# Gated cross-attention and mixture of experts: the reads of the transposed head outputs moved within a slot, ahead of the second pair's exps on ScalarE and ahead of statistics and routing on VectorE

## The chip, the cores and the metric

The kernel runs on 1 core of one Trainium2 chip. The metric is the device time of one execution in microseconds (us), the median of several runs. The time before is 597.08 us (3 runs, 595.59 to 599.96).

## The reference, cut to what matters

Two batches of 1024 tokens of 256 features pass through a gated cross-attention to 154 context rows each (16 heads of 64) and then a gated mixture of experts with top 2 of 8 experts. The kernel works the attention in float32 split in a high and a low part, so that nearly every product is three matmuls.

```python
q = x @ Wq; k = context @ Wk; v = context @ Wv            # 16 heads of 64
attn = softmax(einsum('bhid,bhjd->bhij', q, k) * SCALE)
out = einsum('bhij,bhjd->bhid', attn, v)
x = x + tanh(g_xattn[0]) * (out @ Wo + bo)                # x went in layer-normed
...
logits = clip(xf @ router_w.T, -CLAMP, CLAMP)             # xf: layernorm of layernorm
topk_p, topk_i = top_k(softmax(logits), 2)
x = x + tanh(g_ffn[0]) * sum over chosen experts of down(silu(gate) * up)
```

## The kernel before, in words

**Two phases.** The first phase (a `Block` from L246) does attention and, behind it, routing: it writes the rows chosen for each expert to a queue in HBM. The second phase (L1196 on) runs 39 tiles of 128 queued rows through the experts. The change touches the first phase alone, which takes the first 340 us or so.

**Slots.** The 16 token tiles of 128 rows are worked in NI = 4 iterations of 4 tiles. An iteration has 16 slots, u = 0 to 15, and a slot is one tile's step over four heads (HQ = 4), so a tile takes four slots (UPT = 4). Iteration 0 and iteration 3 are written out, 1 and 2 are passes of a hardware loop (`Fori(1, NI - 1)`). Each engine runs its own `slot(i, u)` with an order of work written by hand, and the engines meet only through semaphores. Everything on one engine is done in the order of its text.

**A slot on TensorE** (L652 to L691) issues: the first half of the scores of slot u + 2 (L543; needs the exps of the first pair of heads of slot u + 1 to be done); the five transposes of the probabilities of slot u (L557); in even slots the four transposes of half of a finished tile's head outputs, `transpose_out` (L590, into a PSUM bank of `O_BANK`); the second half of the scores of slot u + 2 (needs the exps of the second pair of slot u + 1); probabilities times values of slot u - 1, `attend` (L581); a projection job of the next tiles in slots with u % 8 of 0, 1, 2, 4, 5 (L516 and L527, `JOB_SLOT`); `project_out` in slots with u % 4 = 3 (L603, 24 matmuls). The `attend` of an even slot u, which stands in slot u + 1, overwrites the bank that `transpose_out` filled, so it waits on `ot_sb`: for VectorE's read of that bank. In slot 15 the transposes L557 first wait for `pos_read`, the end of VectorE's `count_rows` (L1013), since they overwrite the counts.

**A slot on ScalarE** (L792 to L808): exps of the first pair of heads of slot u + 2 (L773, two activations and their accumulator reads); copy of the transposed probabilities (L800); exps of the second pair of slot u + 2; in even slots `transposed_out` (L779, the cast L782 of the transposed head outputs into `oT_hi`); the high part of a job (L761, L764).

**A slot on VectorE** (L1041 to L1076): the first pair's maxima of slot u + 2 (L892); in odd slots `scale_out` (L901, L903); copy of the rest of the transposed probabilities (L1056); the second pair's maxima; then `block_stats` (u % 4 = 0, L931, L933), `token_stats` (u % 8 = 2, L861, L864), `normalise` (u % 8 = 7), `route_step` (u = 5, 6: `norm_stats` L941, L944; u = 7, 8: `start_output` L970; u = 12, 13: `choose` L997 to L1005), `count_rows` (u = 14, L1010 and L1013); then in even slots `transposed_out` (L911, the subtraction L916 into `oT_lo`, after ScalarE's L782); the low part of a job (L880, L885); the residual (L923) in slots with u % 4 = 3. Iteration 0 has no routing and no `transposed_out` before slot 4.

**Behind it.** GpSimd works the norms of routing (L384 to L407), adds the output bias (L368) and sends rows. In slot 9 TensorE transposes the routed features (L611), ScalarE and VectorE copy them in slot 10 (L786, L974), and the transposes L557 of slot 10 wait for both copies.

Of the kernel before, what the change touches and what calls it, by code (L numbers as in the profile page):

```python
# [47 lines left out]
def gated_xattn_moe(nc, x, ctxT, g_x, g_f, Wq, Wk, Wv, Wo, bo, gamma, beta, rwT, guT, dnT, out):  # L48
# [14 lines left out]
    UPT = H // HQ  # L63
# [25 lines left out]
    with ExitStack() as ctx:  # L89
# [88 lines left out]
        with ExitStack() as actx:  # L178
# [568 lines left out]
            def _(act):  # L747
# [31 lines left out]
                def transposed_out(i, u):  # L779
                    half = (u % UPT) // 2  # L780
                    act.wait_ge(s["ot_ps"][half], TPI * i + u // UPT)
                    nc.scalar.copy(oT_hi[:, 4 * half:4 * half + 4, :].rearrange("p c t -> p (c t)"), O_BANK[half][:, :]).then_inc(s["ot_hi"][half], 1)  # L782

                def turned_features(i):
                    act.wait_ge(s["xfT_ps"], 2 * i - 1)
                    nc.scalar.copy(xfT[:, 0:4, :].rearrange("p c t -> p (c t)"), TA[:, :]).then_inc(s["xfT_sb"][0], 1)  # L786
# [5 lines left out]
                def slot(i, u):  # L792
                    first = isinstance(i, int) and i == 0
                    last = isinstance(i, int) and i == NI - 1
                    if not first and u == TURN + 1:
                        turned_features(i)
                    ahead = exps(i, u + 2) if not (last and u + 2 >= UPI) else iter(())
                    next(ahead, None)
                    act.wait_ge(s["ptA"], UPI * i + u + 1)
                    nc.scalar.copy(pT[u % 2][:, 0:3, :].rearrange("p b t -> p (b t)"), TA[:, 0:3 * P]).then_inc(s["ptA_sb"], 1)  # L800
                    next(ahead, None)
                    if u % 2 == 0 and not (first and u < UPT):
                        transposed_out(i, u)
                    w, g = u % 8, GPI * i + u // 8 + 1
                    if w in JOB_SLOT and not (last and u >= 8):
                        high_part(g, JOB_SLOT[w], JOB_BANK, (u // 8 + 1) % 2)
                    if not first and u == LOGIT + 1:
                        router_exp(i)  # L808
# [14 lines left out]
                for u in range(UPI):  # L823
                    slot(0, u)
# [20 lines left out]
            def _(dve):  # L845
# [65 lines left out]
                def transposed_out(i, u):  # L911

                    half = (u % UPT) // 2
                    part = slice(4 * half, 4 * half + 4)
                    dve.wait_ge(s["ot_hi"][half], TPI * i + u // UPT)
                    nc.vector.tensor_tensor(oT_lo[:, part, :].rearrange("p c t -> p (c t)"), O_BANK[half][:, :],  # L916
                                            oT_hi[:, part, :].rearrange("p c t -> p (c t)").bitcast(F32), ALU.subtract).then_inc(s["ot_sb"][half], 1)
# [123 lines left out]
                def slot(i, u):  # L1041
                    first = isinstance(i, int) and i == 0
                    last = isinstance(i, int) and i == NI - 1
                    w, g = u % 8, GPI * i + u // 8 + 1
                    if not first:
                        route_step_early(i, u)
                    ahead = maxima(i, u + 2) if not (last and u + 2 >= UPI) else iter(())
                    next(ahead, None)
                    if not first and u == LOGIT + 1:
                        shifted_logits(i)  # L1050
                    if not first and u == LOGIT + 2:
                        router_probs(i)
                    if u % 2 == 1 and not (first and u < 2):
                        scale_out(i, u - 2)
                    dve.wait_ge(s["ptB"], UPI * i + u + 1)
                    nc.vector.tensor_copy(pT[u % 2][:, 3:5, :].rearrange("p b t -> p (b t)"), TB[:, 0:2 * P]).then_inc(s["ptB_sb"], 1)  # L1056
                    next(ahead, None)

                    if u % UPT == 0 and u // UPT >= 2:
                        block_stats(i + 1, u // UPT - 2)  # L1060
                    elif u % UPT == 0 and not first:
                        block_stats(i, u // UPT + 2)
                    if w == 2 and not last:
                        token_stats(i + 1, u // 8)
                    if w == 7 and not last:
                        normalise(i + 1, u // 8)
                    if not first:
                        route_step(i, u)
                        if u == COUNT:
                            count_rows(i)  # L1070
                    if u % 2 == 0 and not (first and u < UPT):
                        transposed_out(i, u)
                    if w in JOB_SLOT and not (last and u >= 8):
                        low_part(g, JOB_SLOT[w], JOB_BANK, (u // 8 + 1) % 2)
                    if w % UPT == UPT - 1 and not (first and u < UPT):
                        add_residual(i, u)  # L1076
# [386 lines left out]
```

## Time and profile before

| what | us |
|---|---|
| median of 3 runs | 597.08 |
| the three runs | 597.08, 599.96, 595.59 |
| span of the profiled execution, from its first to its last instruction | 602.2 |
| TensorE busy | 522.3 (87%) |
| VectorE busy | 340.4 (57%) |
| ScalarE busy | 282.2 (47%) |
| GpSimd busy | 231.9 (39%) |

For the profiled execution the page gives the span and no other time. All durations below are from that one execution, core 0, with times counted from the start of its span. PE is TensorE's matmuls, PEld its weight loads, DVE VectorE, ACT ScalarE, POOL GpSimd. In a timeline row the first number is the start, the second the duration, and a bracket at the end tells how long the engine had been idle and what released it. A duration runs from the start to the end of the write, and the next instruction of the same engine can start up to 0.1 us before that end.

### The profile page before, as it was taken

How to read it: one execution, taken by the hardware profiler on the slowest of the kernel's cores; microseconds unless marked ns; L12 is line 12 of the kernel's file. 1: busy time of each engine (PE TensorE's matmuls, PEld its weight loads, DVE VectorE, ACT ScalarE, POOL GpSimd, SP SyncE). 2: the span in 40 equal slices, each digit the busy share in tenths (PEclk: the TensorE clock that was granted, in tenths of full speed). 3: DMA queues.
4: the chain of work that ended last, by engine and by line, in shares of the span. 5: the costliest groups of instructions: out<-in, count | busy, mean ns of one | idle time of the engine just before them, and what ended most of it. 6: DMA issues, size and time to landing. Idle time of an engine off the chain costs nothing.

```text
span 602.2 us, 12363 instructions
## 1 busy us (share of the span) xinstructions
PE 522.3 (87%) x3712; PEld 476.4 (79%) x3713; DVE 340.4 (57%) x783; ACT 282.2 (47%) x866; POOL 231.9 (39%) x319
## 2 busy tenths in 40 slices
PE   8999999999999999998998420699988998999991
PEld 6789999998989889898998410588877877888881
DVE  5856666677586585765756764255444544533330
ACT  3446556555465555564553112355543544533330
POOL 5160000337008780077704625043433433443333
PEclk9999999999999999999999755799999999999995
DMA  8500000001000100001010995636446436333322
GB/s 246 181 2 1 0 2 2 20 1 35 3 0 26 44 20 15 0 10 63 2 36 1 224 229 178 206 84 151 109 90 156 117 76 157 53 51 53 55 36 26
DMA packets 32372, 41.54 MB, mean 69 GB/s; under 512 B 3088, under 2 KB 28432, under 8 KB 32336
## 3 DMA queue, kind: packets, MB, share of 16 engines
q1 hardware_dynamic: 25184, 31.75, 17.9%
q0 software_dynamic: 7152, 9.33, 9.9%
q8 instruction: 21, 0.34, 0.2%
q14 instruction: 15, 0.12, 0.1%
HBM read 24.12 MB, written 16.95 MB: 68 GB/s over the span
## 4 chain that ended last, share of the span: by engine, by line
PE 34%; issue 26%; DVE 11%; ACT 8%; DMA 6%; POOL 6%; POOLq 3%; DVEq 2%; SPq 2%; another core or an unknown queue 1%; ACTq 0%
PE bank L603 7%; PE bank L581 6%; ACT probs L773 5%; PE bank L527 4%; POOL tok L1225 4%; PE bank L543 4%; PE bank L1279 3%; PE bank L557 3%; DMA expert_queue<-zrow 3%; DVE nmax L892 2%; POOLq L1233 2%; DMA out_dram<-yq,to_row 2%; PE bank L706 2%; PE bank L501 2%; DVEq L902 1%
## 5 line engine op out<-in xcount | busy, mean ns | idle before, releaser
L773 ACT ACTIVATE probs<-bank,nmax 128x154 f32<-128x154 f32 x256 | 97.6, 388 | 123.6 <-DVE nmax L892 119.3
L581 PE MATMUL bank<-vdiag,pT 128*128 128x128 f32 (+2 forms) x640 | 80.0, 272 | 7.1 <-DVE oT_lo L916 6.9
L581 PEld LDWEIGHTS bank<-vdiag,pT 128*128 128x128 f32 (+1 forms) x640 | 77.5, 191 | 10.5 <-DVE oT_lo L916 10.3
L1234 POOL DMA_INDIRECT out_dram<-yq,to_row x39 | 61.8, 1585 | 33.7 <-issue 24.1
L1279 PE MATMUL bank<-gu_hi,xqT_hi 128*128 x156 | 68.7, 441 | 1.1 <-DVE xqT_lo L1396 1.1
L892 DVE TENSOR_REDUCE nmax<-bank 128x2 f32<-128x308 f32 x128 | 60.1, 471 | 7.7 <-PE bank L543 6.8
L1279 PE MATMUL bank<-gu_hi,xqT_lo 128*128 x156 | 61.9, 397 | 0.0
L1279 PE MATMUL bank<-gu_lo,xqT_hi 128*128 x156 | 61.7, 396 | 0.0
L1408 DVE TENSOR_TENSOR hidT_lo<-bank,hidT_hi 128x512 fp32r<-128x512 f32 x39 | 26.9, 690 | 53.1 <-ACT hidT_hi L1355 53.1
L1403 DVE TENSOR_TENSOR hid<-hid,bank 128x512 f32<-128x512 f32 x39 | 26.8, 688 | 52.6 <-PE bank L1279 52.6
L557 PE MATMUL bank<-ident,probs 128*128 128x128 f32 (+1 forms) x320 | 46.2, 273 | 5.6 <-ACT xfT L786 2.9
L773 ACT ACTIVATION_READ_ACCUMULATOR probs<-bank,nmax 128x1 f32 x256 | 50.9, 199 | 0.0
L1232 POOL TENSOR_TENSOR to_row<-tok,no_offset 128x1 uint32<-128x1 uint32 x39 | 12.4, 317 | 95.0 <-DMA out_dram<-yq,to_row 90.8
L543 PE MATMUL bank<-k_hi,q_hi 128*128 128x308 f32 x128 | 46.8, 366 | 1.6 <-issue 1.0
L368 POOL TENSOR_TENSOR x<-x,bo_b 128x256 f32<-128x256 f32 (+1 forms) x16 | 12.4, 797 | 91.3 <-DVE xn L871 91.2
L1299 PE MATMUL bank<-dn_hi,hidT_hi 128*128 x156 | 44.4, 284 | 2.2 <-DVE hidT_lo L1408 2.2
L1362 ACT ACTIVATE yq<-bank,tgf 128x256 f32<-128x256 f32 x39 | 18.5, 475 | 55.7 <-DMA out_dram<-yq,to_row 53.8
L1299 PE MATMUL bank<-dn_lo,hidT_hi 128*128 x156 | 44.4, 284 | 0.0
L1299 PE MATMUL bank<-dn_hi,hidT_lo 128*128 x156 | 44.4, 284 | 0.0
L557 PEld LDWEIGHTS bank<-ident,probs 128*128 128x128 f32 (+1 forms) x320 | 37.3, 138 | 7.9 <-ACT xfT L786 3.6
L1262 PE MATMUL bank<-ident,xq 128*128 128x128 f32 x78 | 16.0, 287 | 27.6 <-DMA xq<-expert_queue 27.4
L543 PE MATMUL bank<-k_hi,q_lo 128*128 128x308 f32 x128 | 38.9, 304 | 0.0
(183 smaller groups left out, 1432.4 us busy)
## 6 DMA issues: line engine op xcount, KB each, us to landing
gu_raw<-in_gate_up_wT_dram SPq DMA_DIRECT2D x8, 1024.0 KB, 5.0
expert_queue<-zrow SPq DMA_DIRECT2D x8, 642.5 KB
xq<-expert_queue SPq DMA_DIRECT2D x39, 128.5 KB, 2.5
dn_raw<-in_down_wT_dram SPq DMA_DIRECT2D x8, 512.0 KB, 6.0
x<-in_x_dram SPq DMA_DIRECT2D x4, 512.0 KB, 13.0
out_dram<-out SPq DMA_DIRECT2D x8, 256.0 KB, 2.2
wq_raw<-in_L_xattn_Wq_dram SPq DMA_DIRECT2D x1, 1024.0 KB, 11.5
wo_raw<-in_L_xattn_Wo_dram SPq DMA_DIRECT2D x1, 1024.0 KB, 10.6
```

Source lines behind the costliest of these rows:

```text
L527: last = nc.tensor.matmul(at[:, m * GT:(m + 1) * GT], w[:, c, cols], v[:, c, :], start=(n == 0), stop=(n == 5))
L543: last = nc.tensor.matmul(S_BANK[hf][:, 0:2 * NKB], q[par][:, pair, tok:tok + P], k[:, pair, par, :], start=(n == 0), stop=(n == 2))
L557: last = nc.tensor.transpose(dst, probs[u % 4][:, b * P:b * P + rows], ident[:, :])
L581: last = nc.tensor.matmul(at[:, col0 + j0 * DH:col0 + j0 * DH + n], pT[u % 2][0:rows, b, :], v, start=(b == 0), stop=(b == NBLK - 1), skip ...
L603: last = nc.tensor.matmul(M_BANK[1][:, 0:D], o[:, c, :], w[:, c, :], start=(n == 0), stop=(n == most - 1))
L773: last = nc.scalar.activation(probs[u % 4][:, j * NKB:(j + 1) * NKB], S_BANK[hf][:, m * NKB:(m + 1) * NKB], ACT.Exp, bias=nmax[:, u % 4, j ...
L892: nc.vector.tensor_reduce(nmax[:, u % 4, 2 * hf:2 * hf + 2], S_BANK[hf][:, 0:2 * NKB].rearrange("p (m k) -> p m k", m=2), AX_X, ALU.max, n ...
L1234: nc.gpsimd.indirect_dma_start(out[:, :], bass.IndirectOffsetOnAxis(to_row[:, 0:1], 0), yq[p % 2][:, :], None, compute_op=ALU.add).then_in ...
L1279: last = nc.tensor.matmul(at[p % 2][:, :], rows[:, c, :], weights(w, rank, c * FF2 + half * FF, FF), start=(n == 0), stop=(n == 3 * KD - 1))
L1299: last = nc.tensor.matmul(Y_BANK[p % 2][:, 0:D], h[:, c, :], weights(w, rank, c * D, D), start=(n == 0), stop=(n == 3 * KF - 1))
L1403: nc.vector.tensor_tensor(hid[p % 2][:, :], hid[p % 2][:, :], U_BANK[p % 2][:, :], ALU.mult).then_inc(s["e_hid"], 1)
L1408: nc.vector.tensor_tensor(hidT_lo[:, :, :].rearrange("p c t -> p (c t)"), HT_BANK[:, :], hidT_hi[:, :, :].rearrange("p c t -> p (c t)").bi ...
```

## The change

On both engines the read of the transposed head outputs comes earlier in an even slot. On ScalarE it now stands between the copy L800 and the second pair's exps. On VectorE it now stands directly behind the second pair's maxima, ahead of `block_stats`, `token_stats`, `normalise`, `route_step` and `count_rows`. No instruction is added or removed, no semaphore changes, and TensorE's and GpSimd's programs stay as they are.

```diff
@@ ScalarE, slot(i, u) @@
                     nc.scalar.copy(pT[u % 2][:, 0:3, :]..., TA[:, 0:3 * P]).then_inc(s["ptA_sb"], 1)
-                    next(ahead, None)
                     if u % 2 == 0 and not (first and u < UPT):
                         transposed_out(i, u)
+                    next(ahead, None)
                     w, g = u % 8, GPI * i + u // 8 + 1
@@ VectorE, slot(i, u) @@
                     next(ahead, None)
 
+                    if u % 2 == 0 and not (first and u < UPT):
+                        transposed_out(i, u)
                     if u % UPT == 0 and u // UPT >= 2:
                         block_stats(i + 1, u // UPT - 2)
...
                         if u == COUNT:
                             count_rows(i)
-                    if u % 2 == 0 and not (first and u < UPT):
-                        transposed_out(i, u)
                     if w in JOB_SLOT and not (last and u >= 8):
```

## Rows read from the trace of the kernel before

**Rows 1.** Waits of PE from 42 to 326 us: total, times, longest.

```profile
PE bank L581 <- DVE oT_lo L916: 6.9, 12, 1.4
PE bank L557 <- ACT xfT L786: 2.9, 3, 1.2
PE bank L543 <- ACT probs L773: 0.4, 2, 0.2
```

**Rows 2.** Busy time and count, PE, PEld, DVE, ACT, POOL, then clock, DMA, GB/s.

```profile
42.00:326.00 284.00, 269.18 (x2233) 261.10 (x2234) 190.16 (x498) 161.13 (x630) 104.13 (x131) 1.00 0.04 15
```

**Rows 3.** Timeline of iteration 2, slot 6 and start of 7 (ACT, DVE, PE).

```profile
212.53 0.47 ACT L800 COPY pT<-bank 128x384 f32<-128x384 f32 x1
212.88 0.41 ACT L773 ACTIVATE probs<-bank,nmax 128x154 f32<-128x154 f32 x1
...
213.53 0.22 ACT L773 ACTIVATION_READ_ACCUMULATOR probs<-bank,nmax 128x1 f32 x1
213.62 0.60 ACT L782 CAST oT_hi<-bank 128x512 fp32r<-128x512 f32 x1
...
212.38 0.74 DVE L941 BATCH_NORM_STATS2 stat_b<-xin 128x6 f32<-128x256 f32 x2
...
214.26 0.69 DVE L916 TENSOR_TENSOR oT_lo<-bank,oT_hi 128x512 fp32r<-128x512 f32 x1 [0.82 <-ACT oT_hi L782]
...
213.81 0.41 PE L543 MATMUL bank<-k_hi,q_hi 128*128 128x308 f32 x1
...
215.01 1.33 PE L581 MATMUL bank<-vdiag,pT 128*128 128x64 f32 x10 [0.51 <-DVE oT_lo L916]
```

**Rows 4.** Timeline of iteration 2, slots 8 to 10 (ACT, DVE, POOL, PE).

```profile
221.15 0.47 ACT L800 COPY pT<-bank 128x384 f32<-128x384 f32 x1
...
221.71 0.43 DVE L931 BATCH_NORM_STATS2 stat_b<-x 128x6 f32 x1
...
222.31 1.64 DVE L970 SCALAR_TENSOR_TENSOR out<-xin,tgf,x 128x512 f32<-128x512 f32 x1
...
224.47 0.67 DVE L880 TENSOR_TENSOR xT_lo<-bank,xT_hi 128x512 fp32r<-128x512 f32 x1
...
222.11 1.28 POOL L407 TENSOR_TENSOR xf<-xf,beta_b 128x512 f32<-128x512 f32 x1
223.35 1.86 POOL L368 TENSOR_TENSOR x<-x,bo_b 128x256 f32 x2
...
229.91 0.74 PE L557 MATMUL bank<-ident,probs 128*128 128x128 f32 x5 [1.24 <-ACT xfT L786]
```

**Rows 5.** Timeline of iteration 3, slot 8 (DVE, POOL).

```profile
299.94 0.72 DVE L970 SCALAR_TENSOR_TENSOR out<-xin,tgf,x 128x512 f32<-128x512 f32 x1
...
299.97 1.82 POOL L407 TENSOR_TENSOR xf<-xf,beta_b 128x512 f32<-128x512 f32 x1
```

**Rows 6.** Timeline of iteration 2, slot 13, PE.

```profile
247.26 1.33 PE L581 MATMUL bank<-vdiag,pT 128*128 128x64 f32 x10 [0.39 <-DVE oT_lo L916]
```

**Rows 7.** Timeline of iteration 2, slots 14 and 15 (ACT, DVE, PE).

```profile
253.04 0.48 ACT L800 COPY pT<-bank 128x384 f32<-128x384 f32 x1
...
253.20 0.19 DVE L1010 TENSOR_TENSOR pos<-bank,base_cnt 128x32 f32<-128x32 f32 x1 [0.22 <-PE bank L634]
253.46 0.16 DVE L1013 TENSOR_TENSOR base_cnt<-base_cnt,bank 128x8 f32<-128x8 f32 x1
...
253.76 0.74 PE L557 MATMUL bank<-ident,probs 128*128 128x128 f32 x5
254.32 0.41 PE L543 MATMUL bank<-k_hi,q_hi 128*128 128x308 f32 x1
...
255.52 1.33 PE L581 MATMUL bank<-vdiag,pT 128*128 128x64 f32 x10 [0.51 <-DVE oT_lo L916]
```

**Rows 8.** Timeline of iteration 2, slot 2 (ACT) and start of 3 (PE).

```profile
193.68 0.61 ACT L782 CAST oT_hi<-bank 128x512 fp32r<-128x512 f32 x1
...
194.63 0.39 PE L543 MATMUL bank<-k_hi,q_hi 128*128 128x308 f32 x1
```

## The prediction

> **What bounds the kernel now.** I read the waits of TensorE first, then the busy times of the engines over the stretch that the edit touches, then the timeline slot by slot. Both edits lie in the attention phase. From 42 to 326 us TensorE is busy 269.18 of 284 us at full granted clock, VectorE 190.16 and ScalarE 161.13 [rows 2]. So TensorE sets the time of the phase, and all that any reordering on the other two can give back is what TensorE stands idle: 14.8 us. The reader should see in its waits how that splits: 6.9 us in 12 places are the wait of attend (L581) for VectorE's oT_lo (L916), which is exactly the instruction moved; 2.9 us are the transposes of slot 10 waiting for the copies of the routed features, 0.4 us the scores waiting for exps [rows 1]. At first sight the change is worth 6.9 us, 1.2%. The question is what is late next in each of the 12 places, and what the moved reads push back.
>
> **What the change moves.** Nothing is added or removed. ScalarE's cast L782 keeps its engine for about 0.47 us and gives its place to two exps with accumulator reads, which end 0.47 us later where their maxima are there already; where the maxima are late, the cast fills idle time and costs nothing. On VectorE the subtraction L916 (0.69 us) no longer waits behind statistics; the statistics that used to fill the wait for ScalarE (0.82 us in slot 6 [rows 3]) now come behind it. TensorE's order is untouched, no DMA is moved past another, and GpSimd is touched only through the time of statistics and shared operands. 30 slots carry a moved read; the two reads behind the last iteration (in its tail) are not in a slot and stay. I take the kinds of slot in turn.
>
> *Slots 6 of all iterations and 14 of iteration 0.* ScalarE runs L800 at 212.53, exps at 212.88 to 213.75, cast at 213.62 to 214.22; VectorE subtracts at 214.26 to 214.95; attend starts at 215.01 after 0.51 us of idle time [rows 3]. But the second half of the scores started at 213.81, just as those exps ended (213.53 + 0.22). They need them: they write the bank that the exps read. After the change the cast runs at 212.88, the exps end at 213.75 + 0.47 = 214.22, these scores start at 214.28 instead of 213.81, and attend, about 0.50 us behind their start, at 214.78. The subtraction is done by 214.2. Attend gains 215.01 - 214.78 = 0.23 us, not 0.51: half the wait turns into a wait of L543 for exps. The statistics behind (0.74 us and more) delay the next maxima by 0.3 us; project_out's 3 us hide that. So -0.23 us in each of five places (four slots 6, one slot 14).
>
> *Slot 14 of iterations 1 and 2, the edit's dearest place.* Here count_rows stands behind the moved subtraction. Before, TensorE's counts ended just before 253.20, VectorE read them at once (L1013 ended at 253.62) and the transposes of slot 15, which wait for that, ran at 253.76 [rows 7]. After, VectorE sits in order behind a subtraction that waits for ScalarE: copy at 253.04, cast at 253.40 to 254.00, subtraction at 254.04 to 254.73, counts read from 254.65 and, with the 0.42 us of the two rows, done at 255.07. The transposes start at about 255.13, 1.37 us late; 0.56 us on (the rows' distance to L543) come the scores, 0.50 us on attend, at 256.19 against 255.52. That is +0.67 us, twice. Queued behind the waiting subtraction are count_rows, number_rows and the next maxima; all but the first have slack, since TensorE itself is later. In iteration 3 no exps stand ahead of the cast, and the rows are read about when they were: +0.06.
>
> *Slot 12.* VectorE works choose and then the subtraction without a gap, so attend waits 0.39 us [rows 6] (the like in iteration 1; 1.4 us in iteration 3, the longest of the waits [rows 1]). The subtraction moves ahead of choose, the wait goes. But VectorE has the same work to do up to slot 14, whose first maxima and exps release TensorE again: scores and counts ran together at 253.20 with VectorE busy without a break before. The gain comes back as a later wait; only one drain is saved. I take -0.1 us per iteration 1 to 3.
>
> *Slot 8 of iterations 1 to 3.* The chain that ends the wait of 1.24 us at 229.91 [rows 4] runs on VectorE from slot 8: statistics 221.71, start_output 222.31, subtraction, xT_lo 224.47, and on to the copy of the features. After the change: L800 at 220.92 (0.23 earlier by slot 6), cast to 221.86, subtraction to 222.59, statistics, and start_output wants to begin at 223.29. It lasted 1.64 us in iteration 2 while GpSimd's L407 was running (222.11 to 223.39), and ended 0.56 us behind it; in iteration 3 it had begun 0.03 us before L407, took 0.72 us, and L407 1.82 instead of 1.28 [rows 4, 5]. Whoever begins first holds the other back. So in iterations 1 and 2 it matters whether 223.29 is still inside L407: then start_output ends where it did, the subtraction lies in its shadow, and xT_lo starts 0.60 us earlier. If it misses, the first half of L368 (the pair takes 1.86, some 0.6 a piece net of start_output) holds it to 223.98 and xT_lo starts 0.1 us later. The margin is 0.1 us, less than I can work out. I take -0.25. In iteration 3 the order flips against us: wanted at 300.78, held by L407 until 299.97 + 1.28 = 301.25, ended at 301.85 against 300.66 with the subtraction behind it: the next maxima 0.53 us late, and this chain reaches TensorE: +0.53.
>
> The Trainium skill, page SBUF — State Buffer, section Who interferes with whom, has the rule for this: a VectorE instruction with two SBUF inputs and a GpSimd instruction that reads SBUF block each other for a whole instruction, and issue order decides who waits. The trace agrees (1.64 against 0.72 us, 1.82 against 1.28). Without the rule, with 0.72 us always, slot 8 would give -0.6 us in iterations 1 and 2 and +0.1 in 3, and the sum would be 0.3 us below the old time.
>
> *Slots 0, 2, 4, 10, and 8 of iteration 0.* Here a job follows, so TensorE reaches the next scores later. In slot 2 the exps ended before 193.81 and the next second scores began at 194.63 [rows 8]; 0.47 us later they still come 0.35 us in time. Their statistics get done 0 to 0.3 us later, hidden by the job or project_out. 0, with bounds of -0.1 and +0.1 us in each of some 16 slots.
>
> **The sum.** Slots 6 and 14 of iteration 0: -0.46. Iterations 1 and 2: slot 8, which holds slot 6's gain, -0.25, slot 12 -0.10, slot 14 +0.67, so +0.32 each, +0.64. Iteration 3: +0.53 - 0.10 + 0.06, about +0.5 (again with slot 6 inside). Together +0.7 us. The phase ends on TensorE's work and the expert phase follows unchanged, so this reaches the end one to one. The profiled execution spans 602.2 us, 5.1 above the median of 597.08 and above the slowest run; I carry the difference over: 597.08 + 0.7 = 597.8 us.
>
> **The rivals.**
> *All the waits go.* If attend's wait alone counted: -6.9 us, 590.2 us, 1.2% faster. For it: the wait is the largest in the list. Against it: in slot 6 L543 starts within 0.06 us of the exps' end. 4%.
> *The exps late everywhere.* If the second pair's exps, 0.47 us later, reach TensorE in every one of 30 slots: +14.1 us, 611.2 us, 2.4% slower. It decides from the point where the slack of L543 behind them falls below 0.47 us; in slot 2 it is 0.82, in slots 6 it is 0.06, so it holds in few. 4%.
> *Port order goes wrong in each slot 8,* and the count's wait is full: iterations 1 and 2 give +0.1 instead of -0.25; 598.5 us. 20%, inside no change.
> *It hits in both, and slot 14 is cheaper* because TensorE runs transposes and scores closer: 596 us. 17%.
> The forecast itself (within 0.7 us of 597.8) has 55%.
>
> **How the numbers follow.** A measurement of this kernel tells about 1% (6 us) from no change. Only the first rival passes on the fast side, only the second on the slow side: faster 0.04, same 0.92, slower 0.04. The bounds of the unknown costs are about 2 us either way; the runs before alone spread 4.4 us, and medians can fall apart by some 2 us. 594.7 to 601.3.
>
> **What would show it.** In the waits of TensorE: L581 on oT_lo falls from 6.9 us in 12 places below 1; L543 on ScalarE's exps grows from 0.4 to about 2 us (slots 6: about 0.5 each); L557 on base_cnt (slot 15) appears with 1.3 us twice. The cast L782 starts 0.36 us behind L800. TensorE's busy time in the phase is unchanged and its idle time about 15.5 us. The forecast is wrong if the transposes of slot 15 don't wait over 1 us, or if the idle time of TensorE in the phase changes by over 3 us.

## The result and the profile after

The changed kernel takes 602.21 us (median of 20 runs, 596.14 to 605.83), the kernel before, run beside it, 598.91 us (20 runs, 595.59 to 602.59). The ratio is 1.0047, 95% interval 1.0026 to 1.0068: 2.8 us slower, give or take 1.3. The ratios leave out the few executions that are over 1.5% above the fastest of their kernel (two of the 20 here); the two medians lie 3.3 us apart. The forecast was 597.8 us in 594.7 to 601.3, on a median before of 597.08. So the direction was right, the size a quarter of the measured one, and the time lies above the range. The profiled executions alone would mislead: the changed kernel's spans 597.7 us, less than the 602.2 of before. Where the 4.5 us went stands below.

First two lines of the page of the changed kernel, then its longest waits of TensorE from 42 to 326 us (total, times, longest; the first six), which answer to [rows 1].

```profile
span 597.7 us, 12363 instructions
...
PE 519.4 (87%) x3712; PEld 477.9 (80%) x3713; DVE 340.7 (57%) x783; ACT 281.2 (47%) x866; POOL 229.5 (38%) x319
```

```profile
PE bank L557 <- ACT xfT L786: 3.1, 3, 1.4
PE bank L557 <- DVE base_cnt L1013: 3.0, 3, 1.2
PE bank L543 <- ACT probs L773: 2.1, 6, 0.4
PE bank L557 <- ACT pT L800: 2.0, 1, 2.0
PE bank L611 <- DVE pT L1056: 1.1, 1, 1.1
PE bank L527 <- DVE xT_lo L880: 0.8, 1, 0.8
```

The wait for oT_lo, 6.9 us before, is gone from the list. In its place stand the waits that the forecast named (exps 2.1 us, base_cnt 3.0 us), one of 2.0 us in slot 14 of iteration 3, and two in slots 8 to 10. The wait of slot 10 for the copies of the routed features, 2.9 us before, is 3.1.

**Slot by slot.** The start of the transposes L557 marks each slot on TensorE. I take these 64 starts from the timeline of each kernel and write down how much later (+) or earlier (-) than in the profile of before each slot came, less the same for the slot ahead of it. A figure of 0.28 thus means that the stretch from one slot's transposes to the next took 0.28 us longer. Stretches that differ by under 0.1 us are left out.

```
stretch up to      changed  changed  ScalarE  slot 14  count    changed  slot 8+14
iteration, slot             again    alone    alone    first    filled   as before
0,  8               -0.28    -0.30    -0.29    -0.00    -0.28    -0.28    -0.27
1,  0               -0.30    -0.29    -0.30    -0.01    -0.31    -0.29    -0.30
1,  8               -0.28    -0.27    -0.28     0.00    -0.28    -0.26    -0.27
1, 10               -0.11    -0.12     0.18    -0.03    -0.12    -0.13    -0.92
1, 14               -0.63    -0.63     0.01     0.01    -0.62    -0.62    -0.62
1, 15                1.89     1.92    -0.02     1.34     0.55     1.89     0.54
2,  0               -0.84     0.74    -0.30    -0.83    -0.30    -0.84    -0.30
2,  8               -0.28    -0.28    -0.29     0.00    -0.30    -0.28    -0.29
2, 10                0.62    -0.12    -0.92    -0.84     0.70     0.33     0.10
2, 14               -0.64    -0.64    -0.01     0.02    -0.65    -0.64    -0.64
2, 15                1.90     1.89    -0.02     1.33     0.58     1.90     0.54
3,  0                0.77    -0.83    -0.29    -0.83    -0.29    -0.83    -0.28
3,  8               -0.27    -0.27    -0.28     0.01    -0.28    -0.29    -0.28
3, 10                0.38     0.38    -0.04     0.00     0.38     0.38     0.94
3, 15                0.08     0.07     0.00     0.08     1.64     0.33     1.16
```

(The labels of the columns' kernels, in order: the changed kernel, e9, e1, e4, e3, e12, e10.) What is left out beside small drifts: all seven took 2.0 us less up to slot 5 of iteration 2, 0.3 less up to slot 7, and 1.8 and 0.6 us less up to slots 4 and 5 of iteration 3. So the profiled execution of before had over 4 us of stalls that no other profile has: its timeline shows them as idle time of TensorE put down to "issue", ahead of L557 and L590 at 200 us and of L543 and L557 at 278 us. That is why its span is long; what caused the stalls is not shown.

Three readings come from this table at once. Nearly every slot costs the same to 0.03 us in one kernel after another, so a profile can settle tenths where the times of whole runs, which spread over up to 10 us, can't. The stretches up to slot 10 are the exception: in iteration 2 the changed kernel has +0.62 in one profile and -0.12 in the other. And the stretch behind slot 15 has two values with the same program: -0.84 and +0.77 in the changed kernel's iterations 1 and 2, +0.74 and -0.83 in its second profile. It costs 1.6 us more or it doesn't.

**What differs there is the clock.** The timeline of the changed kernel in slots 14 and 15 of iteration 2 (PE, DVE, ACT), which answers to [rows 7]:

```profile
250.60 0.30 PE L543 MATMUL bank<-k_hi,q_lo 128*128 128x308 f32 x1
252.13 1.05 PE L557 MATMUL bank<-ident,probs 128*128 128x128 f32 x5 [1.22 <-DVE base_cnt L1013]
252.83 0.60 PE L543 MATMUL bank<-k_hi,q_hi 128*128 128x308 f32 x1
...
253.75 2.23 PE L581 MATMUL bank<-vdiag,pT 128*128 128x64 f32 x10
```

```profile
250.05 0.47 ACT L800 COPY pT<-bank 128x384 f32<-128x384 f32 x1
250.41 0.60 ACT L782 CAST oT_hi<-bank 128x512 fp32r<-128x512 f32 x1
```

```profile
251.04 0.69 DVE L916 TENSOR_TENSOR oT_lo<-bank,oT_hi 128x512 fp32r<-128x512 f32 x1 [1.06 <-ACT oT_hi L782]
251.65 0.18 DVE L1010 TENSOR_TENSOR pos<-bank,base_cnt 128x32 f32<-128x32 f32 x1
251.91 0.16 DVE L1013 TENSOR_TENSOR base_cnt<-base_cnt,bank 128x8 f32<-128x8 f32 x1
```

The chain is the one forecast: copy, cast 0.36 us behind it, subtraction 0.03 us behind the cast's end, counts read, transposes. Its end isn't. The five transposes took 1.05 us instead of 0.74 and attend 2.23 instead of 1.33 [rows 7]. The windows of this stretch (busy time of PE, PEld, DVE, ACT, POOL; then the granted clock):

```profile
250.00:251.00 1.00, 0.79 (x7) 0.44 (x3) 0.00 (x0) 1.00 (x5) 0.00 (x0) 1.00 0.00 0
251.00:252.00 1.00, 0.00 (x0) 0.00 (x0) 0.88 (x3) 0.76 (x5) 0.00 (x0) 1.00 0.00 0
252.00:253.00 1.00, 0.87 (x6) 0.87 (x7) 0.93 (x4) 0.47 (x3) 0.00 (x0) 0.73 0.00 0
253.00:254.00 1.00, 1.00 (x6) 1.00 (x6) 0.72 (x3) 0.75 (x4) 0.00 (x0) 0.50 0.00 0
254.00:255.00 1.00, 1.00 (x6) 1.00 (x6) 1.00 (x3) 0.50 (x3) 0.00 (x0) 0.50 0.00 0
255.00:256.00 1.00, 1.00 (x7) 1.00 (x6) 0.77 (x5) 0.35 (x2) 0.68 (x1) 0.56 0.00 0
256.00:257.00 1.00, 1.00 (x10) 1.00 (x10) 0.13 (x1) 0.00 (x0) 1.00 (x3) 1.00 0.08 16
```

TensorE stood idle 1.22 us, and right behind that the granted clock was 0.50, the lower of its two levels (1.2 in place of 2.4 GHz), until past 255, while TensorE was busy without a break. In iteration 1 the same wait (1.23 us) passed at full clock. In the profile of before the clock was 1.00 from 42 to 326 us [rows 2].

That one profile does not make before free of falls. It has a wait of 1.39 us in slot 13 of iteration 3 (L581 on oT_lo), at full clock. In e5, an experiment below in which VectorE's order around this wait is that of before, the clock fell to 0.50 behind the same wait. The row of before, then the row and the window of e5:

```profile
320.81 1.33 PE L581 MATMUL bank<-vdiag,pT 128*128 128x64 f32 x10 [1.39 <-DVE oT_lo L916]
```

```profile
310.50 1.33 PE L581 MATMUL bank<-vdiag,pT 128*128 128x64 f32 x10 [1.38 <-DVE oT_lo L916]
```

```profile
312.00:314.00 2.00, 1.81 (x9) 1.83 (x10) 1.62 (x9) 1.31 (x6) 0.07 (x1) 0.50 0.00 0
```

And behind the last slot, where [rows 2] doesn't reach, every kernel has a wait of 1.49 us for VectorE at L603 (at 334.65 us in before): 14 of the 16 profiles have a low stretch of 3.4 us next to it, those of before and e8 have none. Nor does the length of a wait decide it: slot 10 of iterations 1 and 2 waits 1.0 to 1.4 us in all 16 profiles, and the clock fell behind none of these 32 waits. What else decides stays open.

### The profile page after: what moved, and what is told of

Same layout as the page of the kernel before. It is cut to its first block, busy times and chain, and to the rows that moved or that the text cites. A ratio compares the mean times of both kernels' runs of the same rounds, so it can differ in the third digit from the quotient of the medians.

```text
span 597.7 us, 12363 instructions
## 1 busy us (share of the span) xinstructions
PE 519.4 (87%) x3712; PEld 477.9 (80%) x3713; DVE 340.7 (57%) x783; ACT 281.2 (47%) x866; POOL 229.5 (38%) x319
## 4 chain that ended last, share of the span: by engine, by line
PE 40%; issue 23%; DVE 10%; ACT 7%; DMA 6%; POOL 5%; DVEq 3%; POOLq 2%; SPq 2%; ACTq 0%
PE bank L603 7%; PE bank L581 6%; PE bank L1279 5%; PE bank L543 5%; PE bank L527 5%; ACT probs L773 4%; POOL tok L1225 4%; PE bank L557 3%; DMA expert_queue<-zrow 3%; DVE nmax L892 2%; PE bank L1299 2%; DMA out_dram<-yq,to_row 2%; POOLq L1233 2%; PE bank L706 2%; DVEq L902 2%
## 5 line engine op out<-in xcount | busy, mean ns | idle before, releaser
L581 PE MATMUL bank<-vdiag,pT 128*128 128x128 f32 (+2 forms) x640 | 79.3, 271 | 0.0
L581 PEld LDWEIGHTS bank<-vdiag,pT 128*128 128x128 f32 (+1 forms) x640 | 79.2, 193 | 0.0
L557 PE MATMUL bank<-ident,probs 128*128 128x128 f32 (+1 forms) x320 | 45.9, 274 | 8.9 <-ACT xfT L786 3.1
L543 PE MATMUL bank<-k_hi,q_hi 128*128 128x308 f32 x128 | 47.0, 368 | 2.3 <-ACT probs L773 2.1
L557 PEld LDWEIGHTS bank<-ident,probs 128*128 128x128 f32 (+1 forms) x320 | 37.4, 138 | 10.7 <-ACT xfT L786 3.8
L1362 ACT ACTIVATE yq<-bank,tgf 128x256 f32<-128x256 f32 x39 | 18.5, 474 | 52.8 <-DMA out_dram<-yq,to_row 50.0
L603 PE MATMUL bank<-wo_hi,oT_hi 128*128 128x256 f32 x128 | 38.3, 299 | 1.5 <-DVE oT_lo L916 1.5
```

Source lines behind the costliest of these rows:

```text
L543: last = nc.tensor.matmul(S_BANK[hf][:, 0:2 * NKB], q[par][:, pair, tok:tok + P], k[:, pair, par, :], start=(n == 0), stop=(n == 2))
L557: last = nc.tensor.transpose(dst, probs[u % 4][:, b * P:b * P + rows], ident[:, :])
L581: last = nc.tensor.matmul(at[:, col0 + j0 * DH:col0 + j0 * DH + n], pT[u % 2][0:rows, b, :], v, start=(b == 0), stop=(b == NBLK - 1), skip ...
L603: last = nc.tensor.matmul(M_BANK[1][:, 0:D], o[:, c, :], w[:, c, :], start=(n == 0), stop=(n == most - 1))
```

## The experiments

Each ran beside the kernel before on one chip. "Changed" below means the changed kernel. The fourth column is the ratio of the plain medians of all executions, which differs from the ratio by up to 0.4%. The mean clock is that over a kernel's timed executions, and before's is that of the executions beside it. It takes in the stretch behind slot 15 and the expert phase, whose low stretches differ a little from profile to profile too (41 or 44 us at the start of the expert phase), so it is a coarse measure of the attention phase.

| run | what | ratio (95%) | of medians | mean clock, before's |
|---|---|---|---|---|
| e3 | changed, counts read first | 0.9998 (0.9972 to 1.0024) | 1.0012 | 0.949, 0.954 |
| e4 | before, both moves in slot 14 alone | 1.0018 (0.9989 to 1.0047) | 1.0015 | 0.951, 0.954 |
| e1 | ScalarE's move alone | 0.9962 (0.9939 to 0.9985) | 0.9957 | 0.954, 0.954 |
| e2 | VectorE's move alone | 1.0312 (1.0269 to 1.0355) | 1.0333 | 0.942, 0.954 |
| e7 | changed, gaps filled | 1.0015 (0.9990 to 1.0039) | 1.0020 | 0.955, 0.953 |
| e6 | changed, slot 8 as before | 1.0029 (0.9998 to 1.0060) | 1.0031 | 0.948, 0.953 |
| e8 | before, both moves in slot 8 alone | 1.0031 (1.0008 to 1.0055) | 1.0035 | 0.953, 0.953 |
| e5 | changed, VectorE as before in slots 8, 12, 14 | 0.9969 (0.9946 to 0.9992) | 0.9981 | 0.953, 0.953 |
| e9 | changed, again | 1.0037 (1.0002 to 1.0073) | 1.0036 | 0.947, 0.952 |
| e12 | e7 again | 1.0013 (0.9977 to 1.0048) | 1.0032 | 0.955, 0.952 |
| e10 | changed, slots 8 and 14 as before on VectorE | 0.9962 (0.9926 to 0.9998) | 0.9991 | 0.950, 0.952 |
| e11 | e1, second start_output in slot 11 | 0.9902 (0.9862 to 0.9942) | 0.9940 | 0.951, 0.952 |
| e13 | e2, gaps filled | 1.0255 (1.0208 to 1.0301) | 1.0255 | 0.954, 0.952 |
| e14 | e2 again | 1.0361 (1.0304 to 1.0417) | 1.0376 | 0.941, 0.952 |

**e1 and e2: which of the two edits is it?** e1 has the first hunk of the diff alone, e2 the second.

> Only ScalarE's cast is moved, VectorE's order is that of the kernel before. Theory A: the late exps cost nothing beyond the wait that they replace: slots 6 gain 0.28 us each, slot 14 some 0.3 us each, slot 8 and slot 12 are as before, no wait of L557 on base_cnt in iterations 1 and 2; about 2 us in all, ratio 0.995 to 0.999. Rival B: the cast ahead of the exps is what costs, ratio 1.003 to 1.006.

> Only VectorE's subtraction is moved, ScalarE's order is that of the kernel before. Theory A: the subtraction still waits for the late cast, now with the counts, the statistics and start_output behind it. In slot 14 the transposes of slot 15 start 2.1 us later than before in iterations 1 and 2, attend 1.4 us later, and slot 8's chain loses 1 us in each of iterations 1 to 3; with a falling clock 1.7 us each on top: 6 to 9 us, ratio 1.009 to 1.016. Rival B (VectorE's move is harmless): ratio 0.998 to 1.002.

ScalarE's move alone gains 0.4%, VectorE's alone costs 3.1%, 18.5 us, twice what I had put at the most. Theory A's sign holds in both, rival B falls in both. Together they cost 0.47%, so ScalarE's move takes most of the sting out of VectorE's: behind an early cast the subtraction waits less. In e1 the table shows the pure gain: 0.28 to 0.30 us in each of slots 6 and 14 (the stretches up to 8 and up to 0). In e2 the stretch up to slot 15 took 2.70 us more in iterations 1 and 2 and the one behind it 0.76 more, where I had 2.1 more and then 0.7 less; the stretches up to slots 2, 4, 10 and 14 lose 0.4 to 0.9 us each in iterations 1 and 2, and iteration 3 loses 1.4 up to slot 10, 1.5 up to 14 and 1.95 up to 15. VectorE used to work its statistics while it waited for the cast; in this order they stand behind that wait.

**e3 and e4: slot 14.** e3 changes one condition on VectorE; e4 has the early place on both engines only under `(not first and u == COUNT)`:

```diff
 # e3, VectorE: ahead of the statistics
-                    if u % 2 == 0 and not (first and u < UPT):
+                    if u % 2 == 0 and not (first and u < UPT) and (first or u != COUNT):
                         transposed_out(i, u)
...
 # and behind count_rows, as before
+                    if u % 2 == 0 and not (first and u < UPT) and not ((first or u != COUNT)):
+                        transposed_out(i, u)
```

> The changed kernel, but in slot 14 of iterations 1 to 3 VectorE reads the counts (count_rows) ahead of the moved subtraction, as before. Theory A (the loss is count_rows behind the subtraction: TensorE idles 1.2 us ahead of the transposes of slot 15, and the granted clock may fall behind that gap): the wait of L557 on base_cnt is gone in iterations 1 and 2, the granted clock stays 1.00 from 42 to 326 us, and the time falls 2 to 4 us below the changed kernel's, ratio to the kernel before 0.996 to 1.000. Rival B (the loss is the exps that come 0.47 us late, and slot 8's chain): the time stays within 1 us of the changed kernel's, ratio 1.003 to 1.006.

> The kernel before, with both moves in slot 14 of iterations 1 to 3 alone. Theory A: TensorE idles 1.2 us ahead of the transposes of slot 15 twice, attend there starts 0.4 us or more later, and where the clock falls behind the gap another 1.7 us are lost: ratio 1.003 to 1.009, so most of the loss or more than all of it. Rival B: ratio 1.000 to 1.002, only the 0.4 us per iteration that the slots show.

e3 came out level with before, as theory A has it. Its profile has -0.62, +0.55 and -0.30 us where the changed kernel has -0.63, +1.89 and -0.84: slot 14 gains 0.37 us per iteration in place of losing 0.42. e4's interval takes in both theories; its slots add 1.34 - 0.83 = 0.5 us in each of iterations 1 and 2, and its clock had no fall there in the profile, a mean of 0.951 over the executions. Alone this is less than the whole loss: there had to be another place.

e3 also showed a fall where I had not looked: iteration 3 lost 1.64 us in the stretch up to slot 15. Its timeline of slot 14 (PE), and the windows there:

```profile
315.00 1.28 PE L557 MATMUL bank<-ident,probs 128*128 128x128 f32 x5 [2.01 <-ACT pT L800]
```

```profile
312.00:314.00 2.00, 0.99 (x9) 0.85 (x8) 1.54 (x8) 0.32 (x2) 0.00 (x0) 1.00 0.00 0
314.00:316.00 2.00, 1.00 (x5) 1.03 (x6) 1.77 (x7) 1.63 (x9) 0.00 (x0) 0.76 0.00 0
316.00:318.00 2.00, 2.00 (x12) 2.00 (x11) 0.85 (x4) 1.08 (x4) 1.25 (x2) 0.50 0.03 8
```

So of theory A's three signs one failed: the wait of slot 15 was gone and the time fell, but the clock did not stay at 1.00. Slot 12's gain in iteration 3 does come back as a later wait, as forecast: two waits of 1.4 and 0.4 us became one of 2.0, and the transposes behind them start when they did. Behind the long one the clock fell in two of the five unfilled profiles that have it (e3, e10), behind the one of 1.4 us in one of six (e5).

**e7 and e12: the clock, by filling the gaps.** The added lines, in TensorE's slot ahead of its waits (the waits on proj_sb are for bank M_BANK[0] to be free):

```diff
+                    if not first and (u == COUNT + 1 or (last and u == COUNT)):
+                        if not last:
+                            pe.wait_ge(s["proj_sb"][4], GPI * i + u // 8 + 2)
+                        for _ in range(18 if u == COUNT + 1 else 30):
+                            nc.tensor.matmul(M_BANK[0][:, 0:P], ones[:, :], ones[:, :], start=True, stop=True)
                     if not first and u == COUNT + 1:
                         pe.wait_ge(s["pos_read"], i)
```

> The changed kernel, with matmuls on constants (18, of about 1 us together) that TensorE runs into an unused bank while it waits for count_rows ahead of slot 15's transposes in iterations 1 to 3, and 30 of them in the wait of slot 14 of iteration 3. The waits themselves stay. Theory C (part of the loss is the granted clock, which falls to half for 3.4 us behind such a gap in some executions): no stretch at 0.50 between 42 and 326 us, and 1.5 to 3 us less than the changed kernel, ratio to before 0.999 to 1.002. Rival D (the waits' own length is all): ratio 1.003 to 1.006, as the changed kernel or above it by the extra matmuls.

> The changed kernel with matmuls on constants in the three gaps of slots 14 and 15, once more and now beside the changed kernel itself. Theory C (the clock falls behind the gaps): mean granted clock of the executions above that of the changed kernel, and 1.5 to 3 us less: ratio 0.999 to 1.002. Rival D: within 1 us of the changed kernel, and the same mean clock.

> The changed kernel once more, on the same chip as the three beside it, as their measure. Every theory: ratio 1.003 to 1.007. By the sum of the slots with one fall of the clock in two executions of the gaps: 1.0045.

Nothing is computed faster here, TensorE only does useless work while it waits, and the ratio falls from 1.0047 and 1.0037 (changed, e9) to 1.0015 and 1.0013 (e7, e12), some 1.7 us; by the medians it is 1.2. The intervals overlap, and in the pair that ran side by side, e9 and e12, the medians are 596.84 and 596.60 us: there time alone does not tell theory C from rival D. The clocks hardly overlap: the twelve executions of e12 granted 0.951 to 0.959, those of e9 0.941 to 0.953, and neither filled profile has a low stretch between 42 and 326 us, as theory C wanted, where both profiles of the changed kernel have one. Filled kernels run at a higher mean than before itself (0.952), which fits falls in executions of before too. But the mean clock says more than the time: 0.008 of 597 us is about three stretches of 3.4 us at half clock per execution, where the profiles of the changed kernel have one in the slots. That is left open. The stretches up to slot 15 are the same 1.89 and 1.90 us in e12 as unfilled, so the waits of iterations 1 and 2 are untouched; in iteration 3 the filling itself costs 0.26 us (0.33 against 0.08).

**e13 and e14: the same pair with longer gaps.** In e2 TensorE idles 1.96 us ahead of slot 15's transposes. e13 has 30 such matmuls there, 30 in slot 14 of iteration 3 and 18 in slot 15.

> VectorE's move alone, with 30 matmuls on constants (some 1.7 us) run by TensorE in the 2.0 us wait of slot 15 of iterations 1 and 2, and in slots 14 and 15 of iteration 3. Theory C (the clock falls behind the gap, 1.6 us lost each): no stretch at 0.50 after slot 15, and 3 us or more below the unfilled kernel beside it: ratio 1.022 to 1.027 where that has 1.029 to 1.033. Rival D (the wait is all): within 1 us of the unfilled kernel.

> VectorE's move alone, unfilled, as the measure of the kernel beside it: ratio 1.029 to 1.033, two or more stretches of 3.4 us at 0.50 between 42 and 326 us.

The filled kernel is faster, 1.0255 against 1.0361: 1.06%, some 6 us, with intervals just apart (7 us by the medians): theory C holds, and rival D, which had them within 1 us, falls. The windows behind slot 15 of iteration 1, first of e2, then of e13:

```profile
182.00:184.00 2.00, 1.32 (x8) 1.32 (x9) 1.85 (x7) 0.91 (x5) 0.00 (x0) 0.80 0.00 0
184.00:186.00 2.00, 2.00 (x12) 2.00 (x10) 1.75 (x7) 1.16 (x5) 0.32 (x1) 0.50 0.00 0
```

```profile
180.00:182.00 2.00, 1.73 (x16) 1.64 (x15) 1.85 (x7) 1.22 (x5) 0.00 (x0) 1.00 0.04 8
182.00:184.00 2.00, 2.00 (x19) 2.00 (x19) 1.77 (x7) 0.85 (x4) 0.82 (x2) 1.00 0.00 0
```

The stretch up to slot 15 took +2.70 us in e2 and +2.72 in e13, the one behind it +0.76 and -0.84. In iteration 3 e2's clock was at 0.50 for 10.2 us from 333 us on, and the stretch up to slot 15 took +1.95 against +0.33. e14's profile has three low stretches in the slots, one in iteration 1 and two in iteration 3 (two of the three before 326 us, so its expectation is met); e13's has none. From the first slot to the last e2 and e14 take 4.4 and 4.0 us more than e13. The rest of the 6 us does not stand in the slots and may be scatter of six executions each.

**e8, e6 and e10: slot 8.** e8 is before with both moves in slot 8 of iterations 1 to 3 alone; e6 is changed with VectorE's old order in slot 8; e10 has it in slots 8 and 14. All three are the condition shown for e3, with `u != 8` and `u not in (8, COUNT)` in e6 and e10, and `(not first and u == 8)` on both engines in e8.

> The kernel before, with both moves in slot 8 of iterations 1 to 3 alone. Theory E: start_output begins behind the subtraction and is held by GpSimd; the transposes of slot 10 come 1.4 us later in iteration 2 and 0.4 us later in iteration 3: ratio 1.002 to 1.004. Rival (slot 8 gains as much as it loses): 0.999 to 1.001.

> The changed kernel, but in slot 8 of iterations 1 to 3 VectorE works block_stats and start_output ahead of the subtraction, as before; ScalarE's early cast stays. Theory E (slot 8's start_output falls behind GpSimd's instruction that reads the same memory and drags slot 10 along): slots 8 to 10 of iteration 2 gain about 1.5 us and of iteration 3 about 0.4 us against the changed kernel, 1.9 us in all: ratio 1.000 to 1.003. Rival (only slot 14 costs): 1.003 to 1.006.

> The changed kernel, with VectorE's old order in slot 8 and in slot 14 of iterations 1 to 3; slot 12 stays changed. If the two places are the loss and slot 12 only shifts its wait: ratio 0.995 to 0.999. If slot 12 costs through the one long gap it leaves ahead of slot 14 of iteration 3 (2.0 us in place of 1.4 and 0.4), behind which the clock can fall: 0.998 to 1.002.

e8 is slower by 0.31%, 1.8 us: slot 8 costs by itself, and the rival (up to 1.001) is all but out. Its stretches up to slot 10 are +0.08, -0.16 and +0.85 us, where e4, with slot 8 as before, has -0.03, -0.84 and 0.00: 1.6 us in all, but not split between the iterations as theory E had it. e6 and e10 are less plain. e6 against the changed kernel is 1.0029 to 1.0047 or 1.0037, with overlapping intervals: 0.5 to 1.1 us, less than the 1.9 expected. Its stretches up to slot 10, -0.91, -0.36 and +0.94, show why: it gains in iterations 1 and 2 and loses in 3. e10 as a whole came to 0.9962, inside the first of its two expectations, but its medians give 0.9991, inside the second; which holds is open, and its clock did fall in iteration 3 of its profile (+1.16 up to slot 15).

The rows of the changed kernel in slot 8 of iteration 2 (DVE, POOL), then those of e1 (VectorE's old order), of iteration 1 in before, and of iteration 1 in e5 (old order in slot 8, new in slot 6):

```profile
220.00 1.64 DVE L970 SCALAR_TENSOR_TENSOR out<-xin,tgf,x 128x512 f32<-128x512 f32 x1
221.56 0.68 DVE L880 TENSOR_TENSOR xT_lo<-bank,xT_hi 128x512 fp32r<-128x512 f32 x1
...
219.82 1.27 POOL L407 TENSOR_TENSOR xf<-xf,beta_b 128x512 f32<-128x512 f32 x1
221.05 1.86 POOL L368 TENSOR_TENSOR x<-x,bo_b 128x256 f32 x2
```

```profile
216.47 0.72 DVE L970 SCALAR_TENSOR_TENSOR out<-xin,tgf,x 128x512 f32<-128x512 f32 x1
...
218.48 1.27 POOL L407 TENSOR_TENSOR xf<-xf,beta_b 128x512 f32<-128x512 f32 x1
```

```profile
144.84 1.64 DVE L970 SCALAR_TENSOR_TENSOR out<-xin,tgf,x 128x512 f32<-128x512 f32 x1
...
144.65 1.28 POOL L407 TENSOR_TENSOR xf<-xf,beta_b 128x512 f32<-128x512 f32 x1
```

```profile
141.48 0.72 DVE L970 SCALAR_TENSOR_TENSOR out<-xin,tgf,x 128x512 f32<-128x512 f32 x1
...
141.76 1.59 POOL L407 TENSOR_TENSOR xf<-xf,beta_b 128x512 f32<-128x512 f32 x1
```

In iteration 2 of e1 start_output is done before L407 begins and takes 0.72 us. In the changed kernel it comes 1.2 us later in the slot (4.0 us behind the slot's transposes, against 2.8), falls 0.18 us behind the start of L407 and is held until that ends. The Trainium skill's rule (page SBUF — State Buffer, section Who interferes with whom), that issue order decides who waits, agrees: the same instruction takes 0.72 us ahead of L407 and 1.64 behind its start.

The old place is not free either: iteration 1 of before has start_output held for 1.64 us. Which of the two comes first there goes with the order in the other slots. In the eight profiles with VectorE's new order in those (the changed kernel, e9, e3, e5, e6, e7, e10, e12) L407 begins 3.06 to 3.10 us behind the transposes of slot 8 in iteration 1 and 2.66 to 2.71 in iteration 3; in the five with its old order (before, e1, e4, e8, e11) it is 2.56 to 2.77 and 2.81 to 3.21. (e2, e13 and e14, without ScalarE's move, have 2.5 to 2.7 and 2.9.) By what path is not shown. In iteration 2 it varies with the execution: 3.82 and 3.07 in the two profiles of the changed kernel. In the old order a start_output that is held brings the transposes of slot 10 some 0.9 us later.

**e5: is that all?** VectorE's new order stays in all slots but 8, 12 and 14 of iterations 1 to 3 (the condition of e3 with `(first or u not in (8, 12, COUNT))`).

> The changed kernel, with VectorE's order of the kernel before in slots 8, 12 and 14 of iterations 1 to 3, where routing stands; all other slots and ScalarE as changed. If the loss lies in these three places alone, this equals the kernel with ScalarE's move alone: ratio 0.994 to 0.998, no wait of L557 on base_cnt in iterations 1 and 2. If the statistics behind the subtraction cost in the other slots too: 0.999 to 1.003.

0.9969, against e1's 0.9962: in sum VectorE's move neither gains nor costs in the other slots, and the loss lies in the three places. But it is not without effect there. Up to slot 10 e5 has -0.92, -0.92 and +0.91 us, where e1 has +0.18, -0.92 and -0.04: with VectorE's new order in the other slots L407 comes at another place against slot 8, which frees start_output in iteration 1 and holds it in iteration 3. Its profile also has the fall of the clock behind a wait of before, shown above (1.50 us more up to slot 15 of iteration 3).

**e11: a version that beats both.** ScalarE's move alone, and

```diff
-                    if u in (7, 8):
-                        start_output(i, u - 7)
+                    if u in (7, 11):
+                        start_output(i, (u - 7) // 4)
```

> A version that may beat both: ScalarE's cast early, VectorE's subtraction as before, and the second start_output of iterations 1 to 3 in slot 11 (where VectorE waits for project_out anyway) in place of slot 8. If slot 8's chain on VectorE is what slot 10's transposes wait for, they come 0.7 to 1.6 us earlier in each of iterations 1 and 2, 0.3 us or more in iteration 3: ratio 0.991 to 0.995. If start_output in slot 8 costs nothing by itself: ratio 0.995 to 0.998, as with ScalarE's move alone.

0.9902, 5.8 us below before (3.6 by the medians). Its stretches up to slot 10 are -1.10, -1.08 and -0.73 us, where e1 has +0.18, -0.92 and -0.04. So start_output in slot 8 was costing on TensorE even before, and slot 11 hides it in the wait for project_out. Its waits of TensorE, and start_output in its new place (slot 11 of iteration 2, VectorE):

```profile
PE bank L543 <- ACT probs L773: 2.7, 8, 0.4
PE bank L557 <- ACT xfT L786: 2.4, 3, 1.0
PE bank L581 <- DVE oT_lo L916: 2.1, 3, 1.4
```

```profile
232.53 0.74 DVE L970 SCALAR_TENSOR_TENSOR out<-xin,tgf,x 128x512 f32<-128x512 f32 x1
235.06 0.48 DVE L923 SCALAR_TENSOR_TENSOR x<-bank,tgx,x 128x256 f32 x1 [1.79 <-PE bank L603]
```

## Why the prediction was right in most of its steps and wrong in its size

**Slots 6, and 14 of iteration 0: right.** -0.23 us in each of five places was forecast, -0.27 to -0.30 measured, and the reason holds. The rows of the changed kernel in slots 6 and 7 of iteration 2 (ACT, then PE) answer to [rows 3]: the exps end at 210.99, the scores start at 211.04.

```profile
210.76 0.23 ACT L773 ACTIVATION_READ_ACCUMULATOR probs<-bank,nmax 128x1 f32 x1
...
211.04 0.42 PE L543 MATMUL bank<-k_hi,q_hi 128*128 128x308 f32 x1 [0.38 <-ACT probs L773]
...
211.58 1.22 PE L581 MATMUL bank<-vdiag,pT 128*128 128x64 f32 x10
```

**Slots 12 and 14: right in the wait, blind for what follows it.** Forecast -0.10 + 0.67 = +0.57 us per iteration 1 and 2; at full clock the stretches sum to -0.63 + 1.89 - 0.84 = +0.42. The 1.37 us by which the transposes were to be late is 1.89 - 0.63 = 1.26. The failed step is "attend, at 256.19 against 255.52. That is +0.67 us, twice", which took the rows' durations at full clock for a stretch behind a new gap. With the fall it was 2.03 in iteration 2. The clock was a term that the sum put at nothing, from one profile that showed no fall. The averages of the two changed kernels and of the two filled ones are 1.0042 and 1.0014, so the falls cost about 1.7 us of the loss of 2.5 (1.2 of 2.7 by the medians): about one fall of 1.6 us per execution, as each of the two profiles of the changed kernel has. The unchanged kernel has waits of up to 1.4 us in this phase [rows 1]; I took the full clock behind them for a warrant that none would come, and e5 shows that it can fall there too. The gap ahead of slot 15 stood in my forecast with its length, and the one of 2.0 us in iteration 3 as a gain that "comes back as a later wait", without its length.

**Slot 8: the place of GpSimd's instruction was taken from one profile.** The forecast had start_output begin 4.0 us behind the slot's transposes (3.9 in iteration 3), and it begins 3.99 to 4.0 behind them (3.83). Net of slot 6 it had about 0 in iterations 1 and 2 and +0.76 in 3, +0.7 in sum. The changed kernel has -0.11, +0.62 and +0.38 in one profile and -0.12, -0.12 and +0.38 in the other. What failed is the other half. The sentence "It lasted 1.64 us in iteration 2 while GpSimd's L407 was running" is a true reading, but the sum let L407 stay at 222.11 and 299.97, and took the held start_output for the cost of the old order in every execution. L407 moved: in iteration 3 it began 2.68 us behind the transposes, where the sum had it 3.05 behind them, so start_output was not held and cost half of the forecast. And in iteration 2 the old order is free in e1, e4 and e5. So the loss against a typical execution is larger than against the profile of before: averaged over five profiles with both new orders (changed, e9, e3, e7, e12) the three stretches add +0.6 us, over three of the old order (before, e1, e4) -0.6. That is 1.2 us, with few profiles behind it, where the forecast had 0.7.

**The quiet slots: right in the sum,** by e5 against e1, but the new order in them moves L407, which the forecast left out.

**The first rival** (all waits go, 6.9 us) is excluded by the changed kernel's own time. **The second** (exps late everywhere) too: e1, which has exactly the late exps, is faster. The third, "Port order goes wrong in each slot 8," came nearest, at 598.5 us, and had the sign of what failed, but none of the clock. The fourth, a cheaper slot 14, did not come: the transposes waited 1.22 and 1.23 us. And neither sign of being wrong showed: these waits are over 1 us, and between the first and the last slot TensorE is idle 13.1 us against 14.8. Both signs look at waits, and neither at the clock. One sum in the forecast is off: "the sum would be 0.3 us below the old time" comes to 0.5 by its own terms; nothing rests on it.

**The range** reached 3.5 us above the forecast. The sum as measured would be: slots 6 and 14 of iteration 0, -1.4; slots 12 and 14, +0.9; slot 8, +1.2; clock, +1.2 to 1.7: about +2 us, against 2.8 give or take 1.3. Of the 4.4 us between the forecast and 602.21 us, 1.8 are that the median of before itself came out above the 597.08 of the three runs shown. That part is the luck of three runs; the range had some 2 us for it.

## What to carry to other kernels

Where the engine that sets the time has many short waits, a change that merges them into fewer and longer ones can cost although the idle time stays the same, because the clock may fall behind them (it did here behind 1.22 us in one iteration and not behind 1.23 in another). List the new gaps with their lengths, and try useless matmuls in them, which separates the clock from the wait. In an in-order queue, moving an instruction that waits ahead of short work that another engine needs (here the counts) makes that engine wait too: move the producer (ScalarE's cast) and leave the consumer behind the short work. Where two engines hold each other at shared memory, their relative place must come from more than one execution, and the safest answer is to move the instruction into a slot where its engine waits anyway.

## What was not expected of the hardware

TensorE's granted clock fell from 1.00 to 0.50 behind idle stretches of only 1.2 to 2.0 us inside a phase in which it was otherwise busy, and in some executions not behind the same stretch (1.22 us with a fall, 1.23 us without, in one profile). The kernel before has such a wait too (1.4 us; a fall behind it in e5). Behind slot 15 each fall cost 1.6 us, seen as +0.77 against -0.84 us in the same stretch. In one kernel 18 to 30 matmuls on constants in each gap were worth 1.06% of the time. And an instruction of VectorE that waits for GpSimd in one kernel is free in the next because VectorE's order in other slots was changed (start_output in iteration 1: 1.64 us in before, 0.72 in e5).
